# A fused attention and feed-forward kernel: GpSimd's additions go to VectorE, integer conversions to ScalarE, W_base's statistics to the head, and three engines' programs get another order

## The reference, cut to what matters

```python
h  = einsum('bct,bcd->bdt', x, weights[condition])         # a 64x64 matrix per batch
q, k, v = dequant(h, qw_q, s_q), dequant(h, qw_k, s_k), dequant(h, qw_v, s_v)
# dequant(x, qw, s) = x @ ((qw - 8) * repeat(s, 128, axis=0)), 4-bit values kept as int32
# 32 query heads of 128, 8 key and value heads; rope, causal softmax over 64 positions
x1 = x + dequant(ctx, qw_o, s_o)
c2 = gelu(x1 with W_sess[session] + b_sess) @ W2 + b2       # session matrices, masks by length
out = x1 + c2 @ W_base.T + b_base + LoRA of the two best of 8 experts, by a router
```

## Time and profile before

| | |
|---|---|
| median of 3 runs | 2103.05 us (2101.41 to 2103.34) |
| the profiled execution | 2103.89 us, its span 2102.0 us |
| PE busy | 1774.0 us, 84% |
| VectorE busy | 1669.7 us, 79% |
| ScalarE busy | 1314.9 us, 63% |
| GpSimd busy | 285.4 us, 14% |
| mean granted clock of TensorE | 0.949 |

### The profile page before, as it was taken

How to read it: one execution, slowest core, us unless ns; L and a number is a source line. 1 busy time by engine, 2 the same in 40 slices (tenths; PEclk the granted TensorE clock), 3 DMA queues, 4 the chain that set the end, 5 groups by cost and what they waited for, 6 DMA issues and landing times.

```text
span 2102.0 us, 38872 instructions
## 1 busy us (share of the span) xinstructions
PE 1774.0 (84%) x14306; PEld 945.3 (45%) x14306; DVE 1669.7 (79%) x2675; ACT 1314.9 (63%) x2204; POOL 285.4 (14%) x210
## 2 busy tenths in 40 slices
PE   4789889988998998899889989988909877779999
PEld 3444444444444454444444444544404445555444
DVE  6589989998999899889989988998909966994222
ACT  2557777867776777778677767777707633980000
POOL 0311111111111111111111111111101100330000
PEclk8799999999999999999999999999959988999999
DMA  6210101020001101110200021011211112111111
GB/s 196 69 41 2 55 18 42 6 66 22 22 21 51 43 1 52 22 42 2 71 18 25 22 51 42 2 31 41 52 31 50 61 46 95 42 42 41 41 41 50
DMA packets 119216, 87.68 MB, mean 42 GB/s; under 512 B 13532, under 2 KB 108132, under 8 KB 119012
## 3 DMA queue, kind: packets, MB, share of 16 engines
q1 hardware_dynamic: 118372, 84.83, 13.6%
q10 hardware_dynamic: 640, 0.13, 0.0%
HBM read 76.55 MB, written 8.39 MB: 40 GB/s over the span
## 4 chain that ended last, share of the span: by engine, by line
PE 46%; DVE 27%; issue 12%; DMA 5%; SPq 4%; ACT 4%; DVEq 1%; POOL 0%; ACTq 0%
PE pj L1396 6%; PE pj L1398 5%; DVE y L789 4%; PE cx L1715 4%; PE sa L1462 4%; PE sbk L1462 4%; PE sbk L1464 4%; PE sa L1464 3%; DMA work<-sv_d 3%; DVE work L714 3%; DVE work L712 3%; PE tp L1422 2%; DVE work L702 2%; PE ex L1715 2%; PE sa L1715 2%
## 5 line engine op out<-in xcount | busy, mean ns | idle before, releaser
L1166 ACT ACTIVATE pj<-pj,ratio 128x512 f32<-128x512 f32 x772 | 508.1, 670 | 204.5 <-PE pj L1398 200.3
L1396 PE MATMUL pj<-hid,wts 128*128 128x512 f16 x1024 | 398.6, 389 | 54.7 <-DVE work L714 20.1
L496 POOL TENSOR_TENSOR work<-work 128x512 f32<-128x512 f32 x160 | 229.0, 1431 | 1355.6 <-DVE work L714 1355.6
L1398 PE MATMUL pj<-hid,wts 128*128 128x512 f16 x1024 | 395.4, 386 | 0.0
L1175 ACT ACTIVATE sbk<-sbk,wts 128x512 f32<-128x512 f32 x384 | 256.5, 668 | 163.1 <-PE sbk L1464 140.6
L1175 ACT ACTIVATE sa<-sa,wts 128x512 f32<-128x512 f32 x353 | 235.6, 667 | 78.9 <-PE sa L1464 78.7
L1396 PEld LDWEIGHTS pj<-hid,wts 128*128 128x128 f16 x1024 | 100.8, 98 | 245.1 <-ACT pj L1166 90.1
L1408 PEld LDWEIGHTS tp<-wts,hid 128*128 128x128 f16 x3072 | 182.3, 98 | 30.2
L1408 PE MATMUL tp<-wts,hid 128*128 128x128 f16 x3072 | 192.4, 219 | 0.0
L1462 PE MATMUL sa<-cb,wts 128*128 128x512 f16 x256 | 101.4, 396 | 87.6 <-DVE y L789 85.9
L1166 ACT ACTIVATE ex<-ex,ratio 128x512 f32<-128x512 f32 x224 | 151.6, 677 | 12.4 <-PE ex L1398 11.5
(11 more groups left out here) (241 smaller groups left out, 3348.9 us busy)
## 6 DMA issues: line engine op xcount, KB each, us to landing
wts<-qo_d SPq DMA_DIRECT2D x64, 256.0 KB, 3.0
y<-x_d SPq DMA_DIRECT2D x7, 2048.0 KB, 7.8
wts<-qq_d SPq DMA_DIRECT2D x35, 256.0 KB, 2.9
work<-wb_d SPq DMA_DIRECT2D x32, 256.0 KB, 2.7
int_even<-qq_d SPq DMA_DIRECT2D x29, 256.0 KB, 2.8
out_d<-y SPq DMA_DIRECT2D x12, 512.0 KB, 2.6
work<-qv_d SPq DMA_DIRECT2D x16, 256.0 KB, 6.9
work<-sv_d SPq DMA_DIRECT2D x16, 256.0 KB, 9.1
```

The costliest lines, as they stand in the source:

```text
L496: gp.tensor_tensor(ra[:, u % 2, :], ra[:, u % 2, :], rb[:, :], ALU.add).then_inc(S["rope_sum"], 1)
L1166: act.activation(unit_bank[u][:, :], unit_bank[u][:, :], ACT.Copy, scale=ratio[:, KT * u + j:KT * u + j + 1]).then_inc(u_scaled[u], 1)
L1396: mm(bank[:, :], w_int[:, u, j, :], hid[:, 0, j, CH * c:CH * (c + 1)], start=j == 0, stop=False, skip_group_check=True)
L1398: mm(bank[:, :], w_int[:, u, j, :], hid[:, 1, j, CH * c:CH * (c + 1)], start=False, stop=True, skip_group_check=True).then_inc(u_done[u], 1)
```

## The change

- GpSimd's 160 additions in the steps become `rope_add` on VectorE.
- `int_piece` and `wo_piece` move from VectorE to ScalarE, and stand at five places of ScalarE's step: `pieces(4)` behind the first exponential, `pieces(0)` to `pieces(3)` in the last third. `wo_piece` runs in c = 0, `int_piece` in c = 2, the last pair in c = 3.
- ScalarE rounds unit 2 (`rope_high(ahead, 2)`), VectorE the others. VectorE takes six rescalings a step instead of five.
- W_base's statistics: 8 loads of 512 KB and 8 reductions of 1024 columns, in the head, between the units of step (0, 0).
- The last step's scales come at its end; the small operands and the sessions' mask move to the tail, before the last eight `x1_add`; ScalarE's part of them, too.
- The order of the quanta, rescalings and additions within a step is another in all three programs. PE opens with units 2 and 0 and both lanes; before it was unit 0 and both lanes.
- Four semaphores that counted over all units or halves (`rope_hi`, `qk_ready`, `shifted`) become one for each.

```diff
-WB_STATS = 2 * KT
+WB_STATS = KT
...
+        wb_stage = [work[:, 2048:3072], work[:, 4608:5632]]
...
@@ SyncE, in the head
             load_out_scales(0)
-            for t in range(KT):
+            load_wo(0, 0)
+            load_wo(0, 1)
+            sp.wait_ge(S["w_ready"], PIECES)
+            for k in range(WB_STATS):
+                if k >= 2:
+                    sp.wait_ge(S["wb_read"], k - 1)
+                sp.dma_start(wb_stage[k % 2], w_base_t[P * k:P * (k + 1), :]).then_inc(wb_in[k % 2], 16)
+            for t in range(2, KT):
                 load_wo(0, t)
...
@@ SyncE, behind the loads of w_sess
-            for k in range(WB_STATS):
-                if k >= 2:
-                    sp.wait_ge(S["wb_read"], k - 1)
-                sp.dma_start(w32[:, k % 2, :], w_base_t[P * (k // 2):P * (k // 2 + 1), CH * (k % 2):CH * (k % 2 + 1)]).then_inc(wb_in[k % 2], 16)
...
@@ GpSimd
-            with gp.Fori(0, NC * NKV) as s:
-                for u in range(NU):
-                    gp.wait_ge(S["u_read"], s * NU + (u + 1))
-                    gp.tensor_tensor(ra[:, u % 2, :], ra[:, u % 2, :], rb[:, :], ALU.add).then_inc(S["rope_sum"], 1)
...
@@ VectorE
+            def rope_add(p4, u):
+                dve.wait_ge(S["u_read"], upto(p4, NU, u + 1))
+                dve.tensor_tensor(ra[:, u % 2, :], ra[:, u % 2, :], rb[:, :], ALU.add).then_inc(S["rope_sum"], 1)
...
@@ VectorE, the head's units
             for u in range(NU - 1):
                 rope_cos((0, 0), u)
                 rope_sin((0, 0), u)
-                rope_high((0, 0), u)
+                rope_add((0, 0), u)
+                if u in (0, 1, 3):
+                    rope_high((0, 0), u)
                 rope_split((0, 0), u)
+                for k in (2 * u, 2 * u + 1):
+                    dve.wait_ge(wb_in[k % 2], 16 * (k // 2 + 1))
+                    absmax(wbmax[:, k:k + 1], wb_stage[k % 2]).then_inc(S["wb_read"], 1)
...
@@ ScalarE
+            def int_piece(g, p):
+
+                u, half = p // 2, p % 2
+                act.wait_ge(int_in[p % 2], 16 * NU * g + 16 * (p // 2 + 1 - NU))
+                act.wait_ge(u_done[u], KT * NC * g + (4 * half + 4 - KT))
+                act.activation(w_int[:, u, 4 * half:4 * half + 4, :].rearrange("p k n -> p (k n)"), int_stage[p % 2],
+                               ACT.Copy, bias=-8.0).then_inc(S["int_ready"], 1)
...
@@ ScalarE, the last third of a step
-                ctx_hi(p4, 1)
-                if ahead:
-                    rescale(ahead, 3, 6)
-                if out4:
-                    rescale_out(out4, 7, 2)
-                if ahead:
-                    rescale(ahead, 4, 4)
-                    rescale(ahead, 4, 5)
+                ctx_hi(p4, 1)
+                pieces(1)
+                if out4:
+                    rescale_out(out4, 7, 2)
+                if ahead:
+                    rescale(ahead, 4, 5)
+                if out4:
                     rescale_out(out4, 6, 2)
+                if ahead:
+                    rope_high(ahead, 2)
+                pieces(2)
+                if ahead:
                     rescale(ahead, 4, 6)
+                pieces(3)
```

More of the change, by code:

```diff
@@ L161, in build @@
         u_scaled = [sem(f"u_scaled{u}") for u in range(NU)]
+        rope_hi = [sem(f"rope_hi{u}") for u in range(NU)]
+        qk_ready = [sem(f"qk_ready{u}") for u in range(NU)]
+        shifted = [sem("shifted0"), sem("shifted1")]
         o_done = [sem("o_done0"), sem("o_done1")]
@@ L867, in step @@
                     between("out", 3)
+                if ahead:
+                    rope_add(ahead, 0)
+                soft_norm(p4, 1)
                 pt_copy(p4, 0)
-                if ahead:
-                    rope_sin(ahead, 0)
-                    between("rope", 0)
-                prob_high(p4, 1)
-                prob_split(p4, 1)
                 if ahead:
@@ L917, in group, with out_scales @@
             def group(g, first=False, last=False):
-                def wo_next(what, n):
-                    if what == "out":
-                        wo_piece(g, n)
-                    elif what == "rope" and n == 3:
+                def out_scales(what, n):
+                    if what == "rope" and n == 3:
                         out_inverted(g)
@@ L1297, in next_values, with int_pieces, last_int_pieces, wo_pieces @@
                     dequant_hi(g + 1, 1)
-                def small_highs():
-                    act.wait_ge(S["scales_ready"], 1)
-                    for dst, src, scale in small_parts():
-                        act.activation(dst(0), src, ACT.Copy, scale=scale).then_inc(S["small_hi"], 1)
+                def int_pieces(i):
+                    if i < NU - 1:
+                        int_piece(g + 1, 2 * i)
+                        int_piece(g + 1, 2 * i + 1)
+                def last_int_pieces(i):
+                    if i == NU - 1:
+                        int_piece(g + 1, 2 * i)
+                        int_piece(g + 1, 2 * i + 1)
+                def wo_pieces(i):
+                    if i < NU - 1:
+                        wo_piece(g, 2 * i)
+                        wo_piece(g, 2 * i + 1)
+                def no_pieces(i):
+                    pass
                 for c in range(NC):
+                    pieces = (wo_pieces, no_pieces, no_pieces if last else int_pieces, no_pieces if last else last_int_pieces)[c]
                     ahead = (g, c + 1) if c + 1 < NC else (None if last else (g + 1, 0))
-                    step((g, c), ahead, None if first and c == 0 else (g, c - 1), next_values if c == NC - 1 and not last else nothing)
-                if last:
-                    small_highs()
+                    step((g, c), ahead, None if first and c == 0 else (g, c - 1), next_values if c == NC - 1 and not last else nothing,
+                         pieces)
             for r in range(ROUNDS):
@@ L1527, in step @@
                 if ahead:
-                    quantum(ahead, 1, 2)
-                    quantum(ahead, 0, 7)
+                    quantum(ahead, 2, 5)
+                    quantum(ahead, 1, 5)
                 if out4:
@@ L1616, in step @@
                     quantum(ahead, 4, 6)
+                if out4:
+                    out_quantum(out4, 7, 3)
+                    after(6)
+                    out_quantum(out4, 6, 3)
+                    after(7)
+                if ahead:
                     value_block(ahead, 3)
```

363 lines of the change are left out of this document (180 added, 183 removed).

## The result

The changed kernel takes 1968.34 us, the median of 4 runs (1964.11 to 1974.55), beside 2102.36 for the kernel before: a ratio of 0.9365 with a 95% interval of 0.9335 to 0.9395. That is 134 us less where 82 were forecast, and 14 us under the range. It lies inside rival B's 1957 to 1981.

A forecast was written before the change was run, and what follows sets the result against it. Steps were taken as bound by PE's floor of some 43 us and VectorE, plus one queue-order stall. Span 2102 - 53 (stall) + 2.5 (head) - 32 (steps) = 2019.5, so 2021 us; its own range 2000 to 2040, overall 1982 to 2056.

The forecast's parts named there:

- rival B: Steps: the order pays more, PE's waits for output additions nearly all go, -9 to -12 us a group; chance 0.13.
- part 7: Steps: the new order opens four chains instead of three, cutting PE's weight-load waits by about a third, 6.5 us a group.
- Part 1: Last group's second step: moving W_base's statistics to the head removes the stall, -53 us, bounds -48.8 and -58.
- Rival D: Last step: the stall only moves, since small_stats needs loads of the same queue; 40 us come back, 2061; chance 0.03.
- Part 2: Head: eight W_base reductions between step (0,0)'s units delay VectorE's split by 1.4 us; +2.5 taken, between 0 and +8.
- Parts 3 and 4: VectorE, per group: additions, a rescaling and the moved rounding +15.1 us; conversions moved to ScalarE -3.9 and -9.6.
- Part 5: VectorE: GpSimd's silence ends lengthened instructions; about 22 us come back, 2.8 a group, besides the odd pieces.
- Part 6: Ends of first and third steps: ScalarE's last pair waits about 1.9 us for staging; 1.3 us each charged, 2.5 a group.
- floor: Steps: PE's busy time, some 43 us a step, taken as a limit that no new order gets under.
- Part 8: Tail: moved small operands and sessions' mask, under 4 us, hide in a DMA wait; 0 won, up to 4 if uncovered.
- A: Steps: the stall goes but steps gain nothing, through staging waits or the second step; 2052 to 2072 us; chance 0.20.
- C: Ends of first and third steps: staging waits fully exposed make the kernel slower, 2127 us at 5 us each; chance 0.04.

The follow-up runs named there:

- b_wb: The kernel before with only W_base's statistics moved to the head, out of the last group; 2055 us, ratio 0.9774.
- a_spread: The kernel after with ScalarE's first three pairs of pieces spread over the step, the fourth left at the end; 1933 us, ratio 0.9172.
- b_wb_four: b_wb with unit 2's first four quanta and rescalings early in the step, so four chains open at its beginning; 2058 us, ratio 0.9767.
- a_both_late: a_both_back with unit 2's first five quanta and rescalings a place or two later, three chains at the opening, distances kept; 1978 us, ratio 0.9402.
- a_both_back: The kernel after with additions back on GpSimd and integer conversions back on VectorE, in the new order; 1979 us, ratio 0.9396.
- a_spread_o30: a_spread with tile 3's first rescaling on ScalarE instead of VectorE; 1902 us, ratio 0.9034.
- a_both_three: a_both_back with unit 2's first quanta after the first third of the step, set close together, three chains at the opening; 2127 us, ratio 1.0103.
- a_pieces_back: The kernel after with the integer conversions back on VectorE at the old hooks; 1963 us, ratio 0.9320.

## Why the prediction was wrong

Its direction and its first term held; the step that failed is part 7, "The three programs' order", both in size and in reason.

**Part 1, the stall:** forecast -53, and -50.5 with the head's bill; measured -48 (41 to 54) in b_wb, which holds the head's bill too. Right. Rival D didn't happen.

**Part 2, the head:** forecast +1.4 on VectorE's units, measured +1.0; the opening copy of step (0, 0) comes at 117.3, where it came at 117.2. It was taken as +2.5 with its extras; between +0.2 and +1.0 is what the trace shows.

**Parts 3 and 4, prices:** 0.682, 0.63 and 0.65 us where 0.688 and 0.62 were taken. Right.

**Part 5, the lock:** the lengths vanished as said, L774 runs at 0.679 to 0.691 us throughout. What it is worth in time can't be read from it alone, since it comes together with the additions' own 110 us: the two together won 16 us in either order with the conversions on VectorE, and with them on ScalarE 0 or a few us the wrong way. So in the kernel after, where the conversions had left VectorE too, this term and part 3 together gave nothing that could be measured, and all the new shares together gave 7 us.

**Part 6, ScalarE's staging waits:** the mechanism was right and its place too, since PE waits at unit 2's second quantum in the steps behind the first and third. The size was half: 1.3 us for each of 15 ends, 20 us, where a_spread gave back 41, 2.7 an end. The last pair's wait was right, 1.9 us in the third step; the forecast missed that the third pair waits like the fourth. With 3.6 us in that stretch, the forecast's own sign of being wrong, "3 us or more for staging", came.

**Part 7, the order:** -6.5 us a group was taken, "the lower of these, about a third" of PE's two largest waits, for order and shares together. With part 6 that made -4.0 a group; the kernel after has 134 - 48 = 86 us, 10.8 a group, a little past the forecast's far bound of 10.5. Without the staging waits, as in a_spread, it was 174 - 48 = 126 us, 15.8 a group, of which the order is 79, and the additions and conversions the other 47. So the order's part was mis-sized by itself: 79 us where 52 were put down for order and shares together. Two errors are in it.

The reason, four chains for three, failed in both tests (b_wb_four, a_both_late).

And the bound was drawn from two rows of waits of PE's weight loads, 21 us a group. Those rows don't hold what PE loses in other ways: idle time booked as issue (9.0 us in the same group), and time that the profile counts as busy. From b_wb to a_both_back the span gets 74 us shorter, and PE's idle time only 39 (273 to 234); the other 35 us are PE's busy time, 1774.9 to 1740.2 for the same 14306 matmuls. Part of it can be short pauses that a busy row hides. In b_wb, back to back, the next matmul starts 0.21 to 0.22 us after the last one, but each is booked as 0.38:

```profile
701.49 0.38 PE L1469 MATMUL sbk<-wts 128*128 128x512 f16 x1
701.71 0.38 PE L1471 MATMUL sbk<-wts 128*128 128x512 f16 x1
701.92 0.38 PE L1469 MATMUL sa<-wts 128*128 128x512 f16 x1
702.14 0.38 PE L1471 MATMUL sa<-wts 128*128 128x512 f16 x1
```

So up to 0.16 us of a pause counts as busy. Nor was the forecast's "floor" of some 43 us a step one: PE's busy time in group 3 fell from 171.9 to 169.0 us.

The clock may have a part, but it doesn't decide: the mean granted clock is 0.949 before, 0.959 in b_wb, 0.971 after and 0.976 in a_spread_o30, yet b_wb_four has 0.970 and is no faster than b_wb, and a_both_three has 0.973 and is the slowest run of all.

**Part 8, the end:** forecast 0. From the last step's opening copy to the first Gelu it is 114.5 us before, 111.5 in b_wb and 107.7 after, so about 4 us came from the last step's own order and the moved small operands, which no run parts.

**The rivals:** A is out, since group 3 got 8.3 us shorter. B's time was 1957 to 1981, and its condition came true: PE's waits for the output additions nearly all went, 13.1 to 2.1 us in group 3. Its price of the whole wait held only in the sum, since other waits took part of the place (6.7 us for L813) and other time came back. It was held back by VectorE's busy share, 96% if all came true. VectorE was busy 169.5 of 184.5 us in group 3 after, 92%, and in a_spread_o30 166.0 of 177.0, 94%: a share near that was reached. So a forecast share of 96% was a poor reason to hold B at 0.13. C was the staging wait and would have needed 3.4 us an end beyond what the steps gained; it was 2.7, and the steps gained.

## What to carry to other kernels

Where several engines run programs written out by hand, compare the orders pairwise: if one finishes two banks in the order 5, 4 and the other frees them 4, 5, the exchange of one line can be worth more than moving 110 us of work between engines. Read for every wait of the bounding engine which instruction of its program it is, by its place in the step, and not only which line.

A conversion moved to another engine takes its wait for the load along. Put such pieces as far apart as a load is long, or the receiving engine holds up what stands behind them.

When a term is "a share of the waits", the sum of named waits is a weak upper bound: of the 74 us between b_wb and a_both_back, 35 were booked as PE's busy time before.

Price a moved piece of work beside what else runs on that engine. The same 160 additions won 16 us on VectorE or nothing, depending on whether the conversions were still there.

## What the runs showed of the hardware

ScalarE turned 512 int32 columns to 16 bits in 0.63 to 0.65 us (means of the kernel after) from either staging buffer. VectorE took 0.43 from one, and from the other 1.49 beside a GpSimd addition and 0.42 without (a_both_back, a_pieces_back). With GpSimd silent, VectorE's second part of the probabilities, an instruction with two SBUF inputs, had one length, 0.679 to 0.691 us over 64; before it was up to 1.64. That fits the Trainium skill's "SBUF — State Buffer" (Who interferes with whom), by which either engine blocks the other for a whole instruction. What I hadn't expected is how little it was worth in the kernel after: some 57 us of VectorE's other instructions went when the additions' 109 us came, and the kernel's time moved by nothing that could be measured.
